# First expert network of a two-layer gated-attention kernel: gate and up accumulated over the experts in PSUM, down with tokens on the partitions, each token's expert picked by a per-token factor

## The chip, the cores and the metric

One core of one Trainium2 chip. The number is the device time of one execution in microseconds (us), the median of three.

## The reference

Two layers, each an attention over a context and then a feed-forward block, on 16 x 56 = 896 tokens of width 128. The change is in the feed-forward block of layer 0, a top-1 mixture of 8 routed experts and one shared expert, with inner width 256:

```python
logits = x @ gate_w
top_val = jnp.max(logits, axis=-1, keepdims=True)
top_id = jnp.argmax(logits, axis=-1)
xs = x * jax.nn.sigmoid(top_val)
g = jnp.einsum('th,ehi->eti', xs, rt_gate)
u = jnp.einsum('th,ehi->eti', xs, rt_up)
y = jnp.einsum('eti,eih->eth', jax.nn.silu(g) * u, rt_down)
routed = jnp.einsum('eth,te->th', y, one_hot(top_id, 8))
return silu(x @ sh_gate) * (x @ sh_up) @ sh_down + routed
```

The result is multiplied by tanh(g_ffn[0]) and added to the residual x. Then come the layer norm of layer 1 and its attention, whose queries are made from the normed x.

## The kernel before

Every engine runs an instruction list in the order in which the code writes it. The order is written out by hand, and semaphores (`sem(name)`) carry what one engine needs of another. Names: `pe` TensorE, `act` ScalarE, `dve` VectorE, `pool` GpSimd, `sp` the queue of the DMAs.

Numbers are kept as a float16 high part and a float16 low part (`g_split`, `u_split`, `d_split` for weights, `xs_split`, `xn_split`, `act_split` for data), so a product takes three matmuls: high with high, high with low, low with high. PSUM is `bank`, eight banks of 512 float32 columns.

Before the expert loop stands a head. PE turns the normed x (L747), makes the logits (L1028), and waits while DVE finds the one-hot row of each token. Then it turns the one-hot rows (L1034) and the scored x (L1038), and makes the query bias and output bias of layer 1 with 32 instructions of two columns or one (L1075, L1077).

The expert loop has two halves of the tokens (512 and 384). Within a half it goes over 8 routed experts and the shared one, and over 2 chunks of the inner width (`IC`): 36 units, numbered m. For a routed expert the tokens of the others are set to zero first. `hot_rows` (PE, L1049) spreads one row of the one-hot matrix over the partitions, `hot_mask_out` (ACT, L1391) copies it to SBUF, and `expert_tokens` (POOL, L723) multiplies it into the split x, giving `x_exp`, of which there are two. A unit is then:

- PE: 3 matmuls for gate and 3 for up (L1097), into banks 1, 2 or 3, 4 in turn;
- ACT: silu of the gate bank (L1422); DVE: times the up bank, from PSUM (L1754);
- ACT: high part of the product (`act_high`, L1397); DVE: low part, both inputs in SBUF (`act_low`, L1716);
- PE: 3 matmuls of `down` (L1061) for unit m - 2, issued behind gate and up of unit m, which accumulate in bank 5 (6 for the second half) over all units of the half.

The sum has features on the partitions. ACT copies it out (`block_out`), PE turns it back (L754), and DVE adds it to the residual (L1525). DVE also does the 13 steps `ternary` for the weights of a later network between units, and POOL makes the rstd of the layer norm (L576, L578).

Behind the loop PE makes the queries, 32 matmuls of 448 float32 columns (two instructions each, L1135), the first 16 for the first half of the tokens. ACT and DVE write each out as high and low (L1442, L1769). The norm of the last three token tiles and its turn (`pe_norm_half`) lie among the first 16. Then layer 1's scores begin (`pe_scores1`, L892).

## Time and profile before

| | |
|---|---|
| median of 3 runs | 1237.04 us (1234.59 to 1239.03) |
| the profiled execution's own time | 1237.67 us |
| its span in the trace | 1235.9 us |
| PE busy | 1121.8 us (91% of the span) |
| DVE busy | 890.4 us (72%) |
| ACT busy | 674.8 us (55%) |
| POOL busy | 519.8 us (42%) |
| PE busy from 500 to 600 us | 79.44 us of 100 |
| DVE busy from 500 to 600 us | 71.78 us of 100 |

Busy time is time in which the engine had an instruction under way; that of a matmul includes its passage through the array, so the sum of single durations is larger than the time they take in a row. PEclk is the clock granted to TensorE, 1.00 for 2.4 GHz and 0.50 for 1.2 GHz. The chain of waits is followed back from the last instruction: each piece is what the next one had been waiting for.

### The profile page before, as it was taken

The page shows a single profiled execution, that of the slowest core. Times are in us where ns is not written, and L with a number is a line of the kernel's source. Part 1 is how long each engine was busy: PE and PEld are TensorE (multiplying, and loading weights), DVE is VectorE, ACT ScalarE, POOL GpSimd, SP SyncE. Part 2 cuts the span into 40 slices and gives each one's busy share as a digit, 9 for nine tenths or more (in the row PEclk, how much of TensorE's full clock was granted, in tenths as well). Part 3 has the DMA queues.
Part 4 walks back from the last instruction along what each step waited for, and adds up shares of the span by engine and source line. Part 5 has one row for each costly group of instructions (what it writes and reads, how often), then busy time and mean ns, then how long its engine had stood idle before and what let it go on. Part 6 is the DMA issues. An engine that isn't in the chain of part 4 may idle for free.

```text
span 1235.9 us, 27523 instructions
## 1 busy us (share of the span) xinstructions
PE 1121.8 (91%) x9862; PEld 639.0 (52%) x9864; DVE 890.4 (72%) x1242; ACT 674.8 (55%) x935; POOL 519.8 (42%) x352
## 2 busy tenths in 40 slices
PE   4789999999999979878887999999999999999984
PEld 2255556566665645634433555555555555555542
DVE  7766666666666673587787887878787878878768
ACT  2345555555555545545575656656565656566532
POOL 8546675666666653432213332322232322323220
PEclk9889999999999999699998999999999999999996
DMA  3456555545555461000006887868776776768640
GB/s 105 121 169 197 169 168 165 156 149 160 157 178 158 145 159 47 20 1 26 2 0 130 161 164 142 158 140 163 137 163 144 156 162 141 159 141 160 131 79 16
DMA packets 247351, 157.59 MB, mean 128 GB/s; under 512 B 209664, under 2 KB 220400, under 8 KB 247296
## 3 DMA queue, kind: packets, MB, share of 16 engines
q1 hardware_dynamic: 247008, 156.86, 54.1%
q8 instruction: 34, 0.56, 0.2%
q14 instruction: 21, 0.17, 0.0%
q10 hardware_dynamic: 288, 0.00, 0.0%
HBM read 62.23 MB, written 25.39 MB: 71 GB/s over the span
## 4 chain that ended last, share of the span: by engine, by line
PE 73%; DVE 12%; issue 7%; ACT 6%; DMA 1%; SPq 0%; POOL 0%; ACTq 0%; DVEq 0%; another core or an unknown queue 0%; POOLq 0%
PE bank L892 16%; PE bank L912 15%; PE bank L767 7%; PE bank L791 6%; PE bank L860 5%; PE bank L795 5%; PE bank L808 4%; DVE region L1716 2%; PE bank L868 2%; PE bank L934 2%; DVE neg_max L1573 2%; ACT region L1242 2%; DVE e_row L1534 2%; PE bank L1135 2%; PE bank L1097 2%
## 5 line engine op out<-in xcount | busy, mean ns | idle before, releaser
L1534 DVE CUSTOM_DVE_ANT_0 e_row<-bank,region 112x1500 f32<-112x1500 f32 x128 | 220.1, 1719 | 125.5 <-PE bank L767 124.2
L1242 ACT ACTIVATE region<-bank 125x896 f32<-125x896 f32 x192 | 176.0, 917 | 203.8 <-PE bank L795 203.7
L1573 DVE TENSOR_REDUCE neg_max<-bank 128x1 f32<-128x1500 f32 x112 | 192.6, 1720 | 111.8 <-PE bank L892 111.8
L892 PE MATMUL bank<-region 128*128 128x500 f16 x1008 | 235.3, 379 | 3.2 <-ACT e_row L1269 1.8
L1269 ACT ACTIVATE e_row<-bank,neg_shift 128x1500 f32<-128x1500 f32 x112 | 169.2, 1511 | 101.0 <-DVE neg_shift L1577 58.4
L1278 ACT COPY region<-bank 128x768 f16<-128x768 f16 x192 | 152.4, 794 | 72.3 <-PE bank L860 72.3
L585 POOL CAST u_w<-e_row 128x1500 f16<-128x1500 f32 x56 | 83.0, 1483 | 209.4 <-ACT e_row L1269 179.2
L585 POOL CAST wg_sb<-e_row 128x1500 f16<-128x1500 f32 x56 | 83.1, 1484 | 192.4 <-ACT e_row L1269 128.4
L892 PEld LDWEIGHTS bank<-region 128*128 (+1 forms) x1008 | 97.4, 98 | 108.0 <-issue 3.5
L791 PE MATMUL bank<-row_of,region 112*128 112x448 bf16 x384 | 137.8, 359 | 7.6 <-ACT region L1242 7.6
L795 PE MATMUL bank<-region 97*128 (+1 forms) x768 | 137.6, 260 | 0.0
L912 PE MATMUL bank<-region 125*128 125x384 f16 (+1 forms) x576 | 126.1, 352 | 0.0
L912 PE MATMUL bank<-region,g_w 125*128 125x384 f16 (+1 forms) x576 | 124.8, 352 | 0.2 <-DMA region<-wg_sb 0.2
L646 POOL TENSOR_SCALAR region<-region 112x1500 bf16<-112x1500 int32 x16 | 105.3, 6583 | 35.3 <-PE bank L795 29.2
L767 PE MATMUL bank<-region 96*128 96x500 f16 x384 | 105.9, 385 | 12.5 <-DVE neg_max L1534 6.8
L808 PE MATMUL bank<-region 125*32 125x112 f32 x3072 | 113.1, 266 | 0.0
L795 PEld LDWEIGHTS bank<-region 97*128 97x128 f16 x768 | 76.0, 99 | 43.3 <-issue 0.9
L1600 DVE TENSOR_TENSOR u_w<-e_row,u_w 128x1500 f16<-128x1500 f32 x56 | 95.7, 1709 | 3.2 <-DMA region<-u_w 1.6
L1600 DVE TENSOR_TENSOR wg_sb<-e_row,wg_sb 128x1500 f16<-128x1500 f32 x56 | 95.5, 1706 | 3.1 <-POOL wg_sb L585 3.0
L808 PEld LDWEIGHTS bank<-region 125*32 125x32 f32 x3072 | 67.7, 109 | 41.0 <-issue 34.6
L912 PEld LDWEIGHTS bank<-region,g_w 125*128 125x128 f16 x576 | 52.8, 97 | 38.8 <-issue 1.3
L912 PEld LDWEIGHTS bank<-region 125*128 125x128 f16 x576 | 52.9, 97 | 38.5 <-issue 1.1
(218 smaller groups left out, 1495.3 us busy)
## 6 DMA issues: line engine op xcount, KB each, us to landing
region<-region SPq DMA_DIRECT2D x192, 96.0 KB, 2.2
turned_rows<-region SPq DMA_DIRECT2D x16, 768.0 KB, 3.8
region<-turned_rows SPq DMA_DIRECT2D x32, 384.0 KB, 3.5
c_in<-in_ctx SPq DMA_DIRECT2D x16, 750.0 KB
split_rows<-region SPq DMA_DIRECT2D x16, 750.0 KB
region<-in_mask_Bx1xSxS_if SPq DMA_DIRECT2D x32, 328.1 KB
region<-split_rows SPq DMA_DIRECT2D x24, 250.0 KB
g_w<-split_rows SPq DMA_DIRECT2D x24, 250.0 KB
```

The costliest lines, as they stand in the source:

```text
L585: pool.tensor_copy(halves1[(t + par) % 2][:, 0, :, 0:KP], e_row[(t + par) % 2][:].rearrange("p (c k) -> p c k", c=KC))\
L767: last = pe.matmul(bank[:, k, 0:4 * KP], q0_flat[0:96, bass.ds(b * ROWS + R0 * t, 128)], c_stack[par][0:96, t // 2, 4 * k:4 * k + 4, 0:KP] ...
L791: pe.matmul(into[:, 0:HALF_ROWS], mask_flat[par][:, KP * c:KP * c + 128], row_of[:].rearrange("p h s -> p (h s)"), start=True, stop=False)
L795: last = pe.matmul(into[:, GC * g:GC * (g + 1)], c_stack[par][0:97, 2 * h + g, c, :], q0[0:97, b, rows:rows + GC], start=False, stop=(g == 1))
L808: pe.matmul(bank[32 * j:32 * j + 32, U_BANK, 0:R0], c_pv[par][:, c, 4 * h + j, :], p0[:, c, R0 * j:R0 * (j + 1)], start=(c == 0), stop=False)
L892: last = pe.matmul(score_banks1(par, t)[:, k, :], q1[:, ql, b, 128 * t:128 * (t + 1)], c_t1[par][:, cl, 4 * k:4 * k + 4, 0:KP], start=(ql ...
L912: last = pe.matmul(bank[:, U_BANK, 0:cols], c_keep1[par][:, c, cl, :], p1[grp][0:KP, pl, c, :], start=(c == 0 and cl + pl == 0), stop=(c = ...
L1242: act.activation(p0[:, 2 * i:2 * i + 2, :], ring0("s", h, i)[0:KP, :, 0:HALF_ROWS], ACT.Exp, scale=SCALE0)\
L1269: act.activation(e_row[(t + par) % 2][:].rearrange("p (a k) -> p a k", a=3), score_banks1(par, t), ACT.Exp, bias=neg_shift[:, t:t + 1], ac ...
L1534: dve.tensor_tensor_reduce(out=masked.rearrange("p (a k) -> p a k", a=3), in0=bank[0:R0, 0:3, 0:4 * KP], in1=mask_bias[par][:].rearrange(" ...
L1573: dve.tensor_reduce(neg_max[:, t:t + 1], score_banks1(par, t), AX.XY, ALU.max, negate=True)\
L1600: dve.tensor_tensor(half[:, 1, :, 0:KP], e_row[(t + par) % 2][:].rearrange("p (c k) -> p c k", c=KC), half[:, 0, :, 0:KP], ALU.subtract).t ...
```

## The change

Units are now those of a half, of shared or routed, and of an inner chunk: 8 instead of 36 (`UNITS0`). The shared expert's four come first, two of them ahead of the turn of the one-hot rows. For the routed experts gate and up of all 8 experts accumulate in one pair of banks: only a token's own expert has a non-zero input, so the sum over the experts is that expert's value. silu, product, high and low part are done once for each of the 8 units. `x_exp` is released by a new semaphore, `x_used`.

`down` has the tokens on the partitions now: the product of one tile of 128 tokens is the stationary operand and the down weights of four experts (512 columns) move, then of four more, then of the shared one (128 columns). Each tile thus gets all experts' outputs in banks 5, 6 and 7, and DVE adds the right one to the residual with `pick`: nine dependent instructions for a tile, each multiplying 128 columns by a per-token factor (`hot_g`, zero but for the token's own expert). The four tiles of the first half are done in the second half's expert loop, the last three in the query phase. Copy, turn and addition of the old sum fall away.

```diff
         FFN_HALVES = [(0, 512), (512, NTOK)]
+        UNITS0 = [(half, shared, ic) for shared in (True, False) for half in range(2) for ic in range(IC)]
+        THIRDS = (2, 0, 1)
+        PICKS = NE + 1
+
+        def gate_bank(q):
+
+            return 1 + 2 * (q % 3)
+
+        def act_of(shared, half, ic):
+
+            return act_split[2 * half + ic if shared else 2 * IC + ic]
+
...
+
+            return bank[:, 7, 384:512]
...
             divide0(B - 1, 1, 1)
 
 
-            def low_weights(third):
...
                 a, z = FFN_HALVES[r // NE]
                 pool.wait_ge(sem("hot_mask"), r + 1)
-                if r >= 2:
-                    n = (r - 2) + (r - 2) // NE
-                    pool.wait_ge(sem("up0"), 2 * IC * (n + 1))
+                if r - 2 == NE - 1:
+                    pool.wait_ge(sem("up0"), 2 * 3 * IC)
+                elif r >= 2:
+                    pool.wait_ge(sem("x_used"), r - 1 - (1 if r - 2 >= NE else 0))
...
             for r in range(2 * NE):
-                if r == NE + 6:
-                    pool_rstd(pool, 2, 2 * TT, (0, 4))
                 expert_tokens(r)
+            pool_rstd(pool, 2, 2 * TT, (0, 4))
...
+            def gate_up(q, e, moving, first, last_e, name):
+
+                half, shared, ic = UNITS0[q]
+                a, z = FFN_HALVES[half]
+                if first:
+                    wait(pe, sem("act0"), q - 2)
+                for at, w in ((0, g_split), (1, u_split)):
+                    for wl, xl in ((0, 0), (0, 1), (1, 0)):
+                        last = pe.matmul(bank[:, gate_bank(q) + at, 0:z - a], w[:, e, wl, 128 * ic:128 * (ic + 1)], moving[xl],
+                                         start=(first and wl + xl == 0), stop=(last_e and wl == 1))
+                    if last_e:
+                        last.then_inc(sem("up0"), 1)
+                if name is not None:
+                    last.then_inc(sem(name), 1)
+
...
+            def down(t):
+
+                half = t // 4
+                pe.wait_ge(sem("act_low"), len(UNITS0) - 2 * (1 - half))
+                if t == 0:
+                    pe.wait_ge(sem("d_low"), 3)
+                tok = slice(128 * (t % 4), 128 * (t % 4 + 1))
+                products = [(ic, al, wl) for ic in range(IC) for al, wl in ((0, 0), (0, 1), (1, 0))]
+                for k in range(3):
+                    wait(pe, sem("picked"), PICKS * (t - 1) + (4, 8, 9)[k])
+                    for n, (ic, al, wl) in enumerate(products):
+                        if k < 2:
+                            last = pe.matmul(bank[:, 5 + k, :].rearrange("p (e h) -> p e h", e=4),
+                                             act_of(False, half, ic)[:, al, tok], d_split[:, 4 * k:4 * k + 4, wl, ic, :],
+                                             start=(n == 0), stop=(n == len(products) - 1))
+                        else:
+                            last = pe.matmul(shared_down(), act_of(True, half, ic)[:, al, tok], d_split[:, NE, wl, ic, :],
+                                             start=(n == 0), stop=(n == len(products) - 1))
+                    last.then_inc(sem("down0"), 1)
...
+            pe.wait_ge(sem("xn_t"), 4)
+            pe.wait_ge(sem("gu_low"), 2)
+            shared_unit(0)
             pe.wait_ge(sem("heads_sb"), 8)
+            shared_unit(1)
...
-                half, e = n // (NE + 1), n % (NE + 1)
...
-                for wl, al in ((0, 0), (0, 1), (1, 0)):
-                    last = pe.matmul(bank[:, 5 + half, 0:z - a], d_split[:, e, wl, ic, :], act_split[m % 3][:, al, 0:z - a],
-                                     start=(e == 0 and ic == 0 and wl + al == 0), stop=(e == NE and ic == IC - 1 and wl == 1))
-                last.then_inc(sem("down0"), 1)
...
-            for m in range(UNITS0):
-                n, ic = m // IC, m % IC
...
+            shared_unit(2)
+            hot_rows(1)
+            shared_unit(3)
+            for r in range(2 * NE):
+                half, e = r // NE, r % NE
                 a, z = FFN_HALVES[half]
...
-                wait(pe, sem("act0"), m - 1)
-                for w, at in ((g_split, 0), (u_split, 1)):
...
-                        moving = x_exp[(half * NE + e) % 2][:, xl, 0:z - a] if e < NE else xn_split[:, xl, a:z]
...
-                if m >= 2:
...
+                pe.wait_ge(sem("x_exp"), r + 1)
+                if half == 0 and e in (0, 3):
+                    pe.wait_ge(sem("gu_low"), 2 * (e // 3) + 4)
+                if r + 2 < 2 * NE:
+                    hot_rows(r + 2)
+                moving = [x_exp[r % 2][:, xl, 0:z - a] for xl in range(2)]
+                for ic in range(IC):
+                    gate_up(2 * IC + IC * half + ic, e, moving, e == 0, e == NE - 1,
+                            "x_used" if ic == IC - 1 and e < NE - 1 else None)
+                if r == 2:
                     pe.wait_ge(sem("bias1"), 2)
                     pe.wait_ge(sem("w_abs"), 3)
...
-                if m == 18:
+                if r == NE - 1:
                     turn_ternary(pe, 0)
                     turn_ternary(pe, 1)
-                if m == 20:
+                if r == NE:
...
-                if m == UNITS0 // 2 + 5:
+                if r == NE + 1:
                     pe.wait_ge(sem("w_t"), 3)
-                    pe_block_turn(pe, 2, range(4), in_bank_7)
-                if m == UNITS0 // 2 + 15:
-                    pe_norm_half(pe, range(4))
-            down(UNITS0 - 2)
-            down(UNITS0 - 1)
+                if NE + 1 <= r < NE + 5:
+                    down(r - NE - 1)
+            pe_norm_half(pe, range(4))
...
-                    pe.wait_ge(sem("act0"), UNITS0)
-                if n == 4:
-                    pe_block_turn(pe, 3, range(4, TT), in_bank_7)
+                    pe.wait_ge(sem("act0"), len(UNITS0) - 1)
+                if n == 2:
+                    pe.wait_ge(sem("act0"), len(UNITS0))
+                if n in (3, 5, 7):
+                    down(4 + (n - 3) // 2)
...
+            for n, (a, z) in enumerate(FFN_HALVES):
+                act.copy(xn_split[:, 0, a:z], bank[:, n, 0:z - a]).then_inc(sem("xn_t"), 1)
...
+
+            def silu_out(q):
...
+                act.activation(silu0[:, q % 2, 0:z - a], bank[:, gate_bank(q), 0:z - a], ACT.Silu, scale=1.0 / W_SCALE)\
...
+            def act_high(q):
+                half, shared, ic = UNITS0[q]
+                a, z = FFN_HALVES[half]
+                act.wait_ge(sem("act0"), q + 1)
+                if half == 1 and not shared:
+                    act.wait_ge(sem("down0"), 3 * 4)
+                act.copy(act_of(shared, half, ic)[:, 0, 0:z - a], act0[:, q % 2, 0:z - a]).then_inc(sem("act_high"), 1)
...
+            silu_out(0)
+            silu_out(1)
...
-            for m in range(UNITS0):
...
-                if m % IC == 0 and m // IC + 1 < 2 * (NE + 1):
-                    hot_mask_out(m // IC + 1)
-                if m >= 1:
-                    act_high(m - 1)
...
-                    block_out(0)
-                if m in (19, 21):
...
+            hot_mask_out(1)
+            for q in (2, 3):
+                silu_out(q)
+            for q in (2, 3):
+                act_high(q)
+            act.wait_ge(sem("in_down0"), 32)
+            act.wait_ge(sem("block_ready"), 1)
+            for r in range(2 * NE):
+                if r == NE:
+                    silu_out(4)
+                    silu_out(5)
+                if r + 2 < 2 * NE:
+                    hot_mask_out(r + 2)
+                if 1 <= r < 4:
+                    down_high(r - 1)
+                if r == NE:
+                    act_high(4)
+                    act_high(5)
+                if r in (NE - 1, NE):
+                    for n in ((0, 1), (2,))[r - NE + 1]:
...
+            dve.tensor_scalar(hot_g[:].rearrange("p t e -> p (t e)"), one_hot[:].rearrange("p t e -> p (t e)"),
+                              tanh_g[:, 2:3], 1.0 / W_SCALE, ALU.mult, ALU.mult).then_inc(sem("hot_g"), 1)
+            dve.tensor_scalar(shared_g[:], tanh_g[:, 2:3], 1.0 / W_SCALE, None, ALU.mult).then_inc(sem("hot_g"), 1)
...
+            def act_up(q):
+                a, z = FFN_HALVES[UNITS0[q][0]]
...
+                dve.scalar_tensor_tensor(act0[:, q % 2, 0:z - a], bank[:, gate_bank(q) + 1, 0:z - a], 1.0 / W_SCALE,
+                                         silu0[:, q % 2, 0:z - a], ALU.mult, ALU.mult).then_inc(sem("act0"), 1)
...
+            def act_low(q):
...
+                dve.tensor_tensor(split[:, 1, 0:z - a], act0[:, q % 2, 0:z - a], split[:, 0, 0:z - a],
+                                  ALU.subtract).then_inc(sem("act_low"), 1)
...
+            def down_low(third):
...
+            def pick(t):
...
+                dve.wait_ge(sem("residual"), TT + t)
+                if t == 0:
+                    dve.wait_ge(sem("hot_g"), 2)
+                for e in range(NE + 1):
+                    if e % 4 == 0:
+                        dve.wait_ge(sem("down0"), 3 * t + e // 4 + 1)
+                    if e > 0:
+                        dve.wait_ge(sem("picked"), PICKS * t + e)
+                    source, scale = (of(e), hot_g[:, t, e:e + 1]) if e < NE else (shared_down(), shared_g[:])
+                    done = dve.scalar_tensor_tensor(x_tok[:, t, :], source, scale, x_tok[:, t, :], ALU.mult, ALU.add)
+                    done.then_inc(sem("picked"), 1)
+                dve.wait_ge(sem("picked"), PICKS * (t + 1))
+                dve.sem_inc(sem("residual"), 1)
+
+            act_up(0)
+            act_up(1)
...
+            act_low(0)
+            act_low(1)
+            act_up(2)
+            act_up(3)
+            act_low(2)
+            act_low(3)
...
-            for m in range(UNITS0):
...
-                    ternary(m - 2)
-                if 6 <= m < 16:
-                    ternary(m - 3)
...
-                dve.scalar_tensor_tensor(act0[:, m % 2, 0:z - a], bank[:, 2 + 2 * (m % 2), 0:z - a], 1.0 / W_SCALE,
...
-                if m >= 1:
-                    act_low(m - 1)
-
-                if m == UNITS0 // 2 + 6:
-                    dve_residual(dve, TT + 4, 2, range(4), in_bank_7)
-                    dve_stats(dve, 2, range(4))
-                if m == UNITS0 // 2 + 12:
-                    dve_norm(dve, 2, range(4))
-            act_low(UNITS0 - 1)
+            for step in range(13):
+                ternary(step)
+                if step in (2, 5, 8):
+                    down_low(step // 3)
+            act_up(4)
+            act_up(5)
+            act_low(4)
+            act_low(5)
+            for t in range(4):
+                pick(t)
+            dve_stats(dve, 2, range(4))
+            dve_norm(dve, 2, range(4))
+            act_up(6)
+            act_up(7)
+            act_low(6)
+            act_low(7)
...
-                if n == 4:
-                    dve_residual(dve, 2 * TT, 2, range(4, TT), in_bank_7)
+                if n in (3, 5, 7):
+                    pick(4 + (n - 3) // 2)
+                if n == 7:
                     dve_stats(dve, 2, range(4, TT))
-                if n == 9:
+                if n == 11:
                     dve_norm(dve, 3, range(4, TT))
```

The instruction order around the three places that matter follows. On PE, in the first half of the expert loop, before; L1049 is `hot_rows`, L1097 gate and up, L1061 `down`:

```order
L1049 MATMUL bank<-one_hot_t,expert_row 128x512
L1097 MATMUL bank<-region 128x512 x6
L1061 MATMUL bank<-region 128x512 x3
L1097 MATMUL bank<-region 128x512 x6
L1061 MATMUL bank<-region 128x512 x3
```

and in the changed kernel (L1073 `hot_rows`, L1057 gate and up, L1099 a turn of ternary weights, L1088 and L1092 `down`), from the last expert of the first half on:

```order
L1057 MATMUL bank<-region 128x512 x12
L1099 MATMUL bank<-ident_b,g_w 128x128 x8
L1073 MATMUL bank<-one_hot_t,expert_row 128x384
L1057 MATMUL bank<-region 128x384 x12
L1099 MATMUL bank<-ident_b,g_w 128x128 x4
L1073 MATMUL bank<-one_hot_t,expert_row 128x384
L1057 MATMUL bank<-region 128x384 x12
L1088 MATMUL bank<-region 128x512 x12
L1092 MATMUL bank<-region 128x128 x6
```

No `down` stands between two experts of the first half any more; the first comes behind the second expert of the second half.

On PE in the head (L1028 then L1045 logits, L1034 and L1038 then L1109 and L1113 the two turns, L1057 the shared units), before:

```order
L1028 MATMUL bank<-gate_w_sb,x_norm_t 128x8 x7
L1034 MATMUL bank<-ident,one_hot 8x128 x7
L1038 MATMUL bank<-ident,x_norm 128x128 x7
L1049 MATMUL bank<-one_hot_t,expert_row 128x512
L1075 MATMUL bank<-bq_pad,region 128x2 x8
```

and now:

```order
L1045 MATMUL bank<-gate_w_sb,x_norm_t 128x8 x7
L1057 MATMUL bank<-region 128x512 x12
L1109 MATMUL bank<-ident,one_hot 8x128 x7
L1113 MATMUL bank<-ident,x_norm 128x128 x7
L1073 MATMUL bank<-one_hot_t,expert_row 128x512
L1119 MATMUL bank<-bq_pad,region 128x2 x8
L1121 MATMUL bank<-bv_col,region 128x1 x8
L1057 MATMUL bank<-region 128x384 x6
```

Two shared units of the first half stand between the logits and the turns; the two of the second half follow the biases.

On DVE from the end of the loop into the query phase (L1769, then L1850, is the low part of a query), before:

```order
L1716 TENSOR_TENSOR region<-region 128x384 x2
L1769 SCALAR_TENSOR_TENSOR region<-bank,q_bias,region 128x8x56 x5
L1525 SCALAR_TENSOR_TENSOR x_tok<-bank,tanh_g,x_tok 128x128 x3
L1509 BN_STATS stats<-x_tok 128x6 x3
L1512 BN_AGGR mean_var<-stats 128x2 x3
L1769 SCALAR_TENSOR_TENSOR region<-bank,q_bias,region 128x8x56 x5
```

and now (L1785 is `pick`; ahead of this piece stand the first four tiles' 36 picks and their norm):

```order
L1760 TENSOR_TENSOR region<-region 128x384 x2
L1850 SCALAR_TENSOR_TENSOR region<-bank,q_bias,region 128x8x56 x4
L1785 SCALAR_TENSOR_TENSOR x_tok<-bank,region,x_tok 128x128 x9
L1850 SCALAR_TENSOR_TENSOR region<-bank,q_bias,region 128x8x56 x2
L1785 SCALAR_TENSOR_TENSOR x_tok<-bank,region,x_tok 128x128 x9
L1850 SCALAR_TENSOR_TENSOR region<-bank,q_bias,region 128x8x56 x2
L1785 SCALAR_TENSOR_TENSOR x_tok<-bank,region,x_tok 128x128 x9
L1552 BN_STATS stats<-x_tok 128x6 x3
L1555 BN_AGGR mean_var<-stats 128x2 x3
L1850 SCALAR_TENSOR_TENSOR region<-bank,q_bias,region 128x8x56 x4
```

Three additions became 27 dependent picks in three packets, and the statistics moved from behind the fifth query to behind the eighth.

## Rows read from the trace of the kernel before

**Rows 1.** Busy time by engine, expert loop: window, PE, PEld, DVE, ACT, POOL, PEclk, DMA.
```profile
530.00:540.00 10.00, 7.62 (x34) 3.26 (x35) 8.13 (x13) 4.01 (x9) 2.57 (x2) 1.00 0.00 0
```

**Rows 2.** Chain of waits, 521 to 612 us: start, length, what.
```profile
521.32 4.75 PE bank L1097 x12
...
528.80 2.21 DVE region L1716
531.06 0.82 PE bank L1061 x3
531.88 0.32 PE bank L1049
532.20 0.77 PE bank L1097 x3
...
534.61 2.21 DVE region L1716
...
561.04 1.29 PE bank L1097 x6
...
605.30 0.97 PE bank L1097 x6
```

**Rows 3.** Groups by shape, 521 to 612 us: busy us, mean ns, idle before.
```profile
L1716 DVE TENSOR_TENSOR region<-region 128x512 f16<-128x512 f32 x18 | 23.4, 1300 | 1.6 <-ACT region L1397 1.2
...
L1422 ACT ACTIVATE region<-bank 128x512 f32<-128x512 f32 x18 | 10.7, 597 | 23.9 <-PE bank L1097 23.9
...
L1525 DVE SCALAR_TENSOR_TENSOR x_tok<-bank,tanh_g,x_tok 128x128 f32<-128x128 f32 x4 | 1.1, 335 | 0.0
...
L578 POOL TENSOR_TENSOR rstd<-rstd,half_neg 128x4 f32<-128x4 f32 x1 | 1.0, 1038 | 0.1
```

**Rows 4.** Timeline of DVE and POOL, 515 to 530 us: start, length, instruction.
```profile
515.44 4.60 DVE L1703 SCALAR_TENSOR_TENSOR region<-region 128x768 f16<-128x768 f32 x3
515.60 2.76 POOL L723 TENSOR_TENSOR region<-region 128x1024 f16<-128x1024 f16 x1 [6.38 <-DVE region L1698]
...
523.90 2.12 POOL L723 TENSOR_TENSOR region<-region 128x1024 f16<-128x1024 f16 x1 [5.54 <-ACT region L1391]
524.10 0.69 DVE L1754 SCALAR_TENSOR_TENSOR region<-bank,region 128x512 f32<-128x512 f32 x1 [0.93 <-PE bank L1097]
```

**Rows 5.** Busy time and granted clock (PEclk) in three short windows.
```profile
505.00:506.00 1.00, 1.00 (x7) 1.00 (x6) 0.00 (x0) 1.00 (x3) 1.00 (x2) 0.50 0.00 0
525.00:526.00 1.00, 1.00 (x4) 0.25 (x2) 0.00 (x0) 0.69 (x2) 1.00 (x1) 0.77 0.00 0
526.00:527.00 1.00, 1.00 (x6) 0.42 (x6) 0.82 (x2) 0.41 (x1) 0.02 (x1) 1.00 0.00 0
```

**Rows 6.** Timeline of PE ahead of the loop.
```profile
502.81 0.96 PE L747 MATMUL bank<-ident,x_norm 128*128 128x128 f32 x7 [1.98 <-issue]
...
510.19 1.65 PE L1034 MATMUL bank<-ident,one_hot 128*8 128x128 f32 x7 [2.83 <-DVE one_hot L1685]
...
513.80 3.57 PE L1075 MATMUL bank<-bq_pad,region 128*128 128x2 f32 x16
...
517.23 3.55 PE L1077 MATMUL bank<-bv_col,region 128*128 128x1 f32 x16
```

**Rows 7.** Timeline of two dependent DVE instructions, and of the seven-tile update.
```profile
509.58 0.21 DVE L1683 TENSOR_REDUCE first_top<-is_top 128x7 f32<-128x56 f32 x1
509.82 0.22 DVE L1685 TENSOR_TENSOR one_hot<-expert_id,first_top 128x56 f32<-128x56 f32 x1
...
495.12 1.90 DVE L1525 SCALAR_TENSOR_TENSOR x_tok<-bank,tanh_g,x_tok 128x128 f32<-128x128 f32 x7 [3.37 <-PE bank L754]
```

**Rows 8.** Chain of waits after the loop.
```profile
626.51 12.31 PE bank L1135 x32
...
640.25 2.10 PE bank L892 x9
...
653.65 0.51 PE bank L860 x6
```

More of the change, by code:

```diff
@@ new lines, in shared_unit, with hot_rows @@
+            def shared_unit(q):
+                a, z = FFN_HALVES[UNITS0[q][0]]
+                gate_up(q, NE, [xn_split[:, xl, a:z] for xl in range(2)], True, True, None)
+            def hot_rows(r):
+                half, e = r // NE, r % NE
+                a, z = FFN_HALVES[half]
+                wait(pe, sem("hot_mask"), r)
+                pe.matmul(bank[:, 0, 0:z - a], expert_row[:, e, :], one_hot_t[:, a:z],
+                          start=True, stop=True).then_inc(sem("hot_rows"), 1)
@@ L1031, in _, with turn_ternary @@
+            def turn_ternary(pe, n):
+                pe.wait_ge(sem("w_tern"), n + 1)
+                for j in range(JC):
+                    last = pe.transpose(tern_turned(n)[:, 128 * j:128 * (j + 1)], w_tern[:, n, j, :], ident_b[:])
+                last.then_inc(sem("w_turned"), 1)
+            pe.wait_ge(sem("xn_t"), 4)
+            pe.wait_ge(sem("gu_low"), 2)
+            shared_unit(0)
             pe.wait_ge(sem("heads_sb"), 8)
+            shared_unit(1)
             pe.wait_ge(sem("one_hot"), 1)
@@ L1033, in _ @@
             for t in range(TT):
-                last = pe.transpose(bank[0:NE, t // 4, 128 * (t % 4):128 * (t % 4 + 1)], one_hot[:, t, :], ident[:])
+                last = pe.transpose(bank[0:NE, 7 * (t // 4), 128 * (t % 4):128 * (t % 4 + 1)], one_hot[:, t, :], ident[:])
             last.then_inc(sem("hot_turned"), 1)
@@ L1134, in _ @@
                     pe.wait_ge(sem("q1_low"), n - 3)
-                pe.matmul(bank[:, n % 4, 0:HALF], a1_w[:, h, :], x_norm_t[:, HALF * half:HALF * (half + 1)],
+                pe.matmul(bank[:, 1 + n % 4, 0:HALF], a1_w[:, h, :], x_norm_t[:, HALF * half:HALF * (half + 1)],
                           start=True, stop=True).then_inc(sem("q1_made"), 1)
@@ L1366, in _, with hot_mask_out, down_high @@
             load_table(ACT.Silu)
-            act.wait_ge(sem("in_down0"), 32)
-            act.wait_ge(sem("block_ready"), 1)
-            for third in range(3):
+            def silu_out(q):
+                a, z = FFN_HALVES[UNITS0[q][0]]
+                act.wait_ge(sem("up0"), 2 * q + 1)
+                wait(act, sem("act0"), q - 1)
+                act.activation(silu0[:, q % 2, 0:z - a], bank[:, gate_bank(q), 0:z - a], ACT.Silu, scale=1.0 / W_SCALE)\
+                    .then_inc(sem("silu0"), 1)
+            def act_high(q):
+                half, shared, ic = UNITS0[q]
+                a, z = FFN_HALVES[half]
+                act.wait_ge(sem("act0"), q + 1)
+                if half == 1 and not shared:
+                    act.wait_ge(sem("down0"), 3 * 4)
+                act.copy(act_of(shared, half, ic)[:, 0, 0:z - a], act0[:, q % 2, 0:z - a]).then_inc(sem("act_high"), 1)
+            def hot_mask_out(r):
+                a, z = FFN_HALVES[r // NE]
+                act.wait_ge(sem("hot_rows"), r + 1)
+                wait(act, sem("x_exp"), r - 1)
+                act.copy(hot_mask[r % 2][:, 0:z - a], bank[:, 0, 0:z - a]).then_inc(sem("hot_mask"), 1)
+            def down_high(third):
                 part = slice(3 * third, 3 * third + 3)
@@ L1376, in _ @@
                 cols = 512 if n == 0 else NTOK - 512
-                last = act.copy(one_hot_t[:, 512 * n:512 * n + cols], bank[0:NE, n, 0:cols])
+                last = act.copy(one_hot_t[:, 512 * n:512 * n + cols], bank[0:NE, 7 * n, 0:cols])
             last.then_inc(sem("hot_t"), 1)
@@ L1670, in _ @@
             dve_norm(dve, 1, range(TT))
+            dve.wait_ge(sem("xn_t"), 2)
+            for n, (a, z) in enumerate(FFN_HALVES):
+                dve.tensor_tensor(xn_split[:, 1, a:z], bank[:, n, 0:z - a], xn_split[:, 0, a:z], ALU.subtract)\
+                    .then_inc(sem("xn_t"), 1)
             dve.wait_ge(sem("logits"), 1)
-            dve.tensor_copy(logits[:].rearrange("p t e -> p (t e)"), bank[:, 2, 0:TT * NE]).then_inc(sem("route"), 1)
+            dve.tensor_copy(logits[:].rearrange("p t e -> p (t e)"), bank[:, 7, 0:TT * NE]).then_inc(sem("route"), 1)
             dve.wait_ge(sem("route"), 1)
```

139 lines of the change are left out of this document (39 added, 100 removed).

## The prediction

> **What bounds the kernel now.** The change lies between 500 and 640 us, so I read that stretch and not the shares of the whole span. First the busy time by engine in a stretch of the expert loop [rows 1]: PE works 7.6 of 10 us and DVE 8.1, at the full clock. Neither is full, so something passes from one to the other and waits. Then the chain of waits [rows 2]. The loop's matmuls begin at 521.3 us. From there the chain repeats itself with each routed expert of the first half: DVE's `act_low` (L1716) begins at 528.80 and again at 534.61, a period of 5.81 us. Within it `act_low` takes 2.21 us, and `down` 0.82, the one-hot row 0.32 and half a unit 0.77 hang on it. Where PE is not held up it does six matmuls of 512 columns in 1.29 us (0.215 each) and six of 384 in 0.97 [rows 2]. So an expert needs of PE 3 x 6 x 0.215 + 0.32 = 4.2 us, and 1.6 of the 5.8 are waiting.
>
> Why is `act_low` long? Its mean is 1300 ns over 18, 23.4 us in all [rows 3]; seven at 2.2 us leave some 0.7 for each of the others. The long ones lie beside POOL's multiplication of the next expert's tokens, which takes 2.12 us [rows 4]. An instruction with only one operand in SBUF runs its 0.69 us in the middle of one (524.10 within 523.90 to 526.02) [rows 4]. Three DVE instructions with both operands in SBUF and one POOL instruction together took what they would one after another [rows 4]. DVE and POOL exclude each other for such pairs.
>
> After the loop PE makes the queries: the last 16 take 12.31 us, 0.77 each [rows 8], and layer 1's scores start at 640.25 [rows 8]. That start is what I forecast; after it the programs are alike.
>
> **The change part by part.** Columns on PE stay: gate and up are the same 216 matmuls, and `down` moves 7 x 6 x 1152 = 48,384 columns, as many as 18 x 3 x 896. The gain must come from waits, not from work.
>
> *Head.* Two shared units, 12 matmuls of 512 columns, now stand behind the logits. PE waits 2.83 us there for the one-hot rows [rows 6]. But the clock is at 0.50 (1.2 GHz) there [rows 5], so they take 12 x 512 columns at that clock = 5.1 us: 2.3 us too long for the gap. In return they are dense matmuls, and the one time the clock rose again here was after about 4 us of those: loop from 521.3 [rows 2], 0.77 in the window at 525 and 1.00 in that at 526 [rows 5]. Before that it had stayed at 0.50 through the turns and bias matmuls, in every window between those of the group. So I take it that it rises at the end of the two units. The seven turns (L1034) then cost 0.96 as L747 does at the full clock, not 1.65 [rows 6]: 1.3 us saved with the second seven. The 32 bias instructions take 7.0 us now, 0.22 each [rows 6]; from the turns' ratio, 3.8. Last bias at 520.8 + 2.3 - 1.3 - 3.2 = 518.6. The remaining two shared units (12 x 384 columns) and a row: I assume that the clock falls again during the biases, since it did not rise during them before, so 4.4 us at half speed. First routed expert at 523.0, from when the clock is whole. Bounds: never raised before 523, 527.5; kept, 518.6 + 2.2 = 520.8.
>
> *First half, 8 experts.* Nothing returns from ACT or DVE to PE between experts. PE needs 12 x 0.215 + 0.32 = 2.9 us for one. POOL's multiplication for expert r + 2 may start when r's matmuls are done, and has the 2.9 us of r + 1: 2.12 and some 0.3 for signals fit, by 0.5. DVE meanwhile does the 13 `ternary` steps and three `down_low`, which exclude POOL now and then; I add 1.0 us, and 0.2 for the sum over the weights. 23.2 + 1.2: end T = 547.4. Upper bound for this cost, every multiplication delayed by a whole DVE instruction of 0.87 (4.60 less the 2.0 in which POOL had it, by three) [rows 4]: 3.3 us an expert, 3 us more in all.
>
> *Turnover.* ACT stands before silu of the first sum in its own queue: it waits for eight ternary turns (0.7 us) and copies them out (two at 0.6, as [rows 3] has for 512 columns), then silu 0.6, DVE's product 0.69 [rows 4]. PE meanwhile has 0.26 + 0.97 and then must wait for the product, as the fourth pair of banks is the first again: 1.4 us. With 0.97, four turns, a row and 1.95 for the second expert: T + 7.1 = 554.5. The low parts are ready then, also with POOL once in the way.
>
> *Four tiles of `down` with three experts between.* A tile is 12 x 0.215 + 6 x 0.085 (six turns of 128 columns in 0.51 [rows 8]) = 3.1 us. An expert of the second half is 12 x 0.162 + 0.26 = 2.2. 12.4 + 6.6: 573.5. DVE's nine picks a tile depend on each other. One such instruction takes 0.335 us [rows 3], and a dependent one starts 0.03 after its predecessor ends (509.58 + 0.21, then 509.82) [rows 7]: 0.365, 3.3 us a tile. PE comes back to the same banks 2.2 us after leaving them, and the pick starts while PE is in the second bank, so this stays hidden.
>
> *To the queries.* Three experts, 6.4 us. POOL must do the last multiplication before the rstd of 1.04 us [rows 3], DVE the norm, PE four turns, ACT a copy: 1.3 us behind the experts. 581.2.
>
> *Queries.* 32 x 0.77 = 24.6 us, three tiles of `down` 9.3, the second norm's turn and copy 1.2, from the last query to the scores 1.4 (626.51 + 12.31 to 640.25 [rows 8]). And three new waits. DVE's list has the pick behind query 3, 5 and 7, PE's has `down` ahead of these queries and the next `down` waiting for four picks: PE stands 2.2 us before the second tile and 2.2 before the third. Then pick and statistics of the third hold back DVE's low parts, and PE waits 3.5 us for a bank at query 12. Sum 44.5 with small gaps. Scores at 625.7.
>
> 640.25 - 625.7 = 14.5 us less. The profiled execution took 1237.67, the median is 1237.04; I take it from the median: **1222.5**.
>
> The Trainium skill, "VectorE: DVE Perf Modes", section on the TRN2 errata, speaks against the picks: an instruction pays a fixed cost, from PSUM 120 cycles beside one per column, so tiles should have 512 columns or more. By that a pick would be 258 ns, which is the pitch of independent ones here (1.90 us for seven [rows 7]). For dependent ones the row of 335 ns decides, 23 us of DVE for 63 picks instead of 16.
>
> The skill's "SBUF - State Buffer", section "Who interferes with whom", says that an instruction of DVE with two SBUF inputs and one of GpSimd that reads SBUF exclude each other for their whole length. The trace agrees: 2.12 against 2.76 us for the same multiplication [rows 4]. By it no pick can be held up by POOL, since its source is in PSUM.
>
> **The rivals.**
>
> *The clock in the head comes out otherwise.* It does not rise early: +4.5, 1227.0, chance 0.15. For it: it stayed low for 20 us once. Or it rises and is kept: -2.2, and with fewer delays by DVE another -1, 1219.3, chance 0.15.
>
> *Picks overlap,* if a dependent one starts at the independent pitch of 0.26: 0.95 us a tile for the three tiles that PE waits for, -2.8, 1219.7. Chance 0.06; against it stand the dependent pairs.
>
> *POOL sets the pace of the first half* at 3.3 us an expert, and waits of PE on the one-hot rows come with it (each needs the mask before it copied, by an ACT that now also copies down weights): +3 to +5, 1226.5. Chance 0.08. For it: the margin is 0.5 us. Against it: DVE's list of such instructions is short.
>
> *The pick chain becomes the bound, and the kernel slower.* Its place is the second half, where a tile's chain stands against 5.3 us of PE, and the query phase, where PE waits for it. With a pitch p the query phase costs 27 (p - 0.365) more, and from p = 0.58 on the four tiles cost 36 (p - 0.58) more. The gain of 14.5 is gone at p = 0.72, twice the row; at 0.8 it is 5 us slower, 1242. For it: 63 instructions with a semaphore each, reading banks while PE writes their neighbours. Against it: L1754 reads PSUM under the same circumstances in its usual 0.69. Chance 0.05.
>
> *The buffers don't decouple:* if an expert's mask, multiplication and matmuls stay in series, 0.6 + 2.1 + 2.6 + signals is again 5.6 us and nothing is won in the first half: 1244 at worst. The order speaks against it, as the row for r + 2 is issued ahead of r. Chance 0.02.
>
> **How the numbers follow.** The forecast, 1222.5, has 0.49. Its own uncertainty is 3 us to each side. Down, the cases near 1219 with both small gains together reach 1216; up, the slow clock and the delays of POOL reach 1229. Between 1216 and 1229 I count some 0.8 of the chance. Below lie sums in which every wait is shorter, above the last two rivals. 0.3% of this kernel is 3.7 us, about what its measurement can tell from no change; to be within it the gain would have to lose 11 us, more than clock and POOL together. Faster 0.92, the same 0.03, slower 0.05.
>
> **What would show it.** In the changed trace: PEclk back at 1.00 before the biases; gate and up of the first half's experts at a period of 2.9 us with DVE and ACT no longer in the chain; one wait of some 1.4 us at the turnover; picks at a pitch of 0.365; PE waits of 2.2, 2.2 and 3.5 us among queries 5, 7 and 12; scores at 626. I am wrong if the period in the first half is over 3.3, if the query phase is over 50 us, or if the change shifts the clock's falls in layer 1 by more than 2 us.

## The result

The changed kernel takes 1222.38 us (median of 4, 1221.34 to 1223.59) against 1237.51 (median of 4, 1234.59 to 1239.03): ratio 0.9868, 95% interval 0.9826 to 0.9909, 15.1 us less; 1222.5 was forecast. The profiled execution has a span of 1219.7 us. PE is busy for 1116.7 us of it, DVE for 868.9 (890.4 before), ACT for 647.7 (674.8). All medians here leave out one slow execution, of `a_three_picks` (1875.6 us at a mean granted clock of 0.56).

The stretch of [rows 1] in the changed kernel (columns as there: window, PE, PEld, DVE, ACT, POOL, PEclk, DMA):

```profile
530.00:540.00 10.00, 9.97 (x45) 3.95 (x44) 9.90 (x9) 2.68 (x5) 7.53 (x4) 1.00 0.00 1
```

PE went from 7.6 of 10 us to 9.97. DVE reads 9.9, but it no longer holds PE up: part of that reading is its own waiting behind POOL, as the groups between 520 and 545 us tell (busy us, mean ns):

```profile
L741 POOL TENSOR_TENSOR region<-region 128x1024 f16<-128x1024 f16 x7 | 15.8, 2252 | 9.1 <-PE bank L1057 6.7 <-ACT region L1425 2.4
...
L1829 DVE TENSOR_SCALAR g_w<-g_w 128x512 bf16<-128x512 f32 x3 | 5.1, 1707 | 0.0
```

L1829 is the `ternary` step, which takes 0.43 us where POOL leaves it alone (the last of the three, at 543.72) and 2.35 us twice, beside POOL's multiplication. Nobody waits for it. POOL's multiplication has a mean of 2252 ns: five of the seven take 2.12 or 2.13 us, and two, beside DVE instructions with both inputs in SBUF, 2.54 and 2.60.

The chain of waits of the changed kernel, which answers to [rows 2] and [rows 8]:

```profile
501.00 0.64 PE bank L764 x4
...
505.54 4.87 PE bank L1057 x12
...
520.50 2.70 PE bank L1057 x12
523.20 0.32 PE bank L1073
523.52 2.70 PE bank L1057 x12
526.21 0.32 PE bank L1073
526.53 2.70 PE bank L1057 x12
...
544.40 0.46 PE bank L1099 x8
...
546.49 0.70 DVE region L1752
...
550.93 2.59 PE bank L1088 x12
...
569.59 0.26 PE bank L1073
...
577.56 2.52 PE bank L1170 x6
...
604.53 4.99 PE bank L1170 x8
...
624.34 2.10 PE bank L909 x9
```

No DVE or ACT piece stands between the experts, whose period is 3.01 us (520.50, 523.52, 526.53) against 5.81. DVE comes in once at the turnover (546.49). Read from the first turn of the normed x (501.00; 502.81 in [rows 6], 1.8 us earlier here, although the program up to there did not change: in the kept executions of this and the other kernels below it comes anywhere from 500.9 to 504.6), against the working of the prediction:

| us from the first turn | forecast | measured |
|---|---|---|
| last bias done | 15.8 | 15.3 |
| first routed expert | 20.2 | 19.5 |
| first half done (T) | 44.6 | 43.4 |
| first tile of `down` | 51.7 | 49.9 |
| four tiles done | 70.7 | 68.6 |
| first query | 78.4 | 76.6 |
| layer 1's scores | 122.9 | 123.3 |

In the kernel before the last was 137.4. So 14.1 us of the two spans' 16.2 come from the changed stretch. The 1.8 us before it are spread between executions, and from the scores to the end the two are 0.3 us apart (595.4 and 595.7).

### The profile page after: what moved, and what is told of

Read it like the earlier page. It is cut to its first block, busy times and chain, and to the rows that moved or that the text cites. A ratio compares the mean times of both kernels' runs of the same rounds, so it can differ in the third digit from the quotient of the medians.

```text
span 1219.7 us, 27431 instructions
## 1 busy us (share of the span) xinstructions
PE 1116.7 (92%) x9875; PEld 634.8 (52%) x9875; DVE 868.9 (71%) x1244; ACT 647.7 (53%) x878; POOL 520.5 (43%) x352
## 4 chain that ended last, share of the span: by engine, by line
PE 76%; DVE 10%; issue 7%; ACT 5%; DMA 1%; SPq 0%; POOL 0%; ACTq 0%; DVEq 0%; POOLq 0%
PE bank L909 16%; PE bank L929 16%; PE bank L784 7%; PE bank L808 6%; PE bank L877 5%; PE bank L812 5%; PE bank L825 4%; PE bank L1057 4%; DVE e_row L1577 2%; PE bank L885 2%; DVE neg_max L1616 2%; ACT region L1277 2%; PE bank L951 2%; PE bank L1170 2%; PE bank L855 2%
## 5 line engine op out<-in xcount | busy, mean ns | idle before, releaser
L784 PE MATMUL bank<-region 96*128 96x500 f16 x384 | 106.1, 386 | 12.3 <-DVE neg_max L1577 6.8
L812 PEld LDWEIGHTS bank<-region 97*128 97x128 f16 x768 | 76.0, 99 | 43.4 <-issue 0.9
```

What stands on the lines that cost most here:

```text
L784: last = pe.matmul(bank[:, k, 0:4 * KP], q0_flat[0:96, bass.ds(b * ROWS + R0 * t, 128)], c_stack[par][0:96, t // 2, 4 * k:4 * k + 4, 0:KP] ...
L812: last = pe.matmul(into[:, GC * g:GC * (g + 1)], c_stack[par][0:97, 2 * h + g, c, :], q0[0:97, b, rows:rows + GC], start=False, stop=(g == 1))
```

## Experiments

**The exclusion taken out of the kernel before** (`b_no_multiply`; part of the computation is left out):

```diff
-                pool.tensor_tensor(x_exp[r % 2][:, :, 0:z - a], xs_split[:, :, a:z], ...
+                c = z - a if r < 2 else 8
+                pool.tensor_tensor(x_exp[r % 2][:, :, 0:c], xs_split[:, :, a:a + c], ...
```

> The kernel before, with POOL's multiplication of the expert's tokens cut to 8 columns from the third on (the semaphores stay, most of x_exp keeps old data, so part of the computation is left out). Theory: the 1.6 us of waiting per expert in the first half is act_low shut out by that multiplication (2.21 us instead of 0.68). Then the period falls from 5.81 to about 4.3 us, all L1716 take 0.5 to 0.7 us, and the kernel takes 1217 us (7 x 1.5 + 8 x 1.2 = 20 less). Rival: the waiting is the round trip PE, ACT, DVE, PE itself; then the period stays over 5 us and the time over 1230 us.

1220.58 us, ratio 0.9831 (0.976 to 0.9902). The chain of waits for one expert:

```profile
526.18 0.32 PE bank L1050
526.50 1.40 PE bank L1098 x6
527.90 0.65 PE bank L1062 x3
528.55 1.29 PE bank L1098 x6
529.85 0.65 PE bank L1062 x3
530.49 0.32 PE bank L1050
```

PE follows PE; the period is 4.3 us, and act_low fell from a mean of 1300 ns to 686. 36 units, every silu and every low part, the round trip over three engines are still there. So that trip fits into PE's time, and the 1.6 us of waiting were POOL's: the cut takes its time and its exclusion together, and since no POOL piece stands in the chain of the kernel before [rows 2], it is the exclusion that counts. The gain is 17 us and not 20: where the second half makes the norm, the chain still goes over DVE (its updates, statistics and low parts, 573 to 578 us and 584 to 588 us in this kernel) in two of the experts.

**The same cut in the changed kernel** (`a_no_multiply`; same diff, part of the computation left out):

> The changed kernel with POOL's multiplication cut to 8 columns from the third on (part of the computation is left out). In the kernel before this same cut gave 17 us. Theory: the change had already taken that wait away, only some 1 us of POOL remains (the norm behind the last multiplication, one wait at an expert): 1221 us. Rival: the two are separate gains, and the cut is worth 17 us here too (1205).

1222.51 us, ratio 0.9873 (0.9806 to 0.9941): no change against 1222.4, though the four executions lie between 1218.2 and 1226.8. The trace is sharper. The first half lasts 23.8 us (23.9 with the multiplication), and from there to the first query it is 32.6 instead of 33.2: POOL is worth some 0.7 us here, and not 17. The two don't add up: the change had taken away the wait that the cut takes away.

**POOL's work doubled** (`a_double_multiply`):

```diff
-                pool.tensor_tensor(x_exp[r % 2][:, :, 0:z - a], ...
+                for twice in range(2):
+                    done = pool.tensor_tensor(x_exp[r % 2][:, :, 0:z - a], ...
+                    done.then_inc(sem("x_exp" if twice else "x_exp_once"), 1)
+                    if not twice:
+                        pool.wait_ge(sem("x_exp_once"), r + 1)
```

> The changed kernel with POOL doing each multiplication of the expert's tokens twice. Theory: an expert of the first half has 3.0 us of PE for 2.12 + 0.3 us of POOL; twice the multiplication is 4.3 + 0.3, so the period becomes 4.6 and PE waits for POOL in the first half, 7 x 1.6 us, and some 2 us in the last experts: 1235 us. Rival: PE doesn't follow POOL that closely because two buffers give it two periods; then under 1227 us.

1242.57 us (median of 10, 1235.65 to 1253.52), ratio 1.0034 (0.9994 to 1.0074), 20 us above the changed kernel where 13 were expected. POOL now is in the chain (start, length, what):

```profile
530.23 2.13 POOL region L742
...
534.50 2.13 POOL region L742
...
553.91 4.30 PE bank L1061 x12
```

The mechanism is as expected, and within the stretch the size nearly so: from the first turn to the scores it is 137.8 us instead of 123.3, 14.4 more. Of these the first half has 12.3 (36.2 instead of 23.9). Its period is 4.3 to 5.0 us, with a POOL that is itself held up beside DVE (its instructions take up to 2.72 us), and the clock is at 0.50 in the window from 554 to 556 us, so that the last expert of the half takes 4.30 us of matmuls instead of 2.7. The other 6 of the 20 us lie outside the stretch, 2.0 before it and 3.8 after the scores in this execution; nothing here shows why. The prediction's margin of 0.5 us is what this loop must keep: POOL's time beyond it comes back as time of the kernel.

**The shared units back behind the biases** (`a_shared_late`):

```diff
             last.then_inc(sem("logits"), 1)
-            shared_unit(0)
             pe.wait_ge(sem("heads_sb"), 8)
-            shared_unit(1)
             pe.wait_ge(sem("one_hot"), 1)
...
             pe.wait_ge(sem("xs_t"), 4)
+            shared_unit(0)
+            shared_unit(1)
             shared_unit(2)
...
-            silu_out(0)
-            silu_out(1)
...
+            silu_out(0)
+            silu_out(1)
             act_high(0)
```

ACT's silus move behind its copies with them, as shown, and DVE's two products (`act_up`) behind the low part of the scored x.

> The changed kernel, with the shared expert's first two units moved from between logits and turns to behind the bias matmuls. Theory: these two units fill PE's wait for the one-hot rows and bring the clock back before the turns and biases; without them turns and biases take 1.65 and 7.0 us again, and the first routed expert starts 6 us later than in the changed kernel: 1228.5 us. Rival: in front they cost as much as they save (5.1 us of half speed against a gap of 2.8), so the time stays within 2 us of 1222.4.

1227.7 us, ratio 0.9917 (0.9881 to 0.9952): 5.3 us more than the changed kernel. But this is a median between two groups: five executions took 1224.5 to 1225.7 us and five 1229.7 to 1237.0. All ten lie above 1224.4, which goes against the rival; that the total is 6 us more, no run shows. The kept trace is the fastest execution. Its chain:

```profile
508.24 1.65 PE bank L1107 x7
...
511.92 3.50 PE bank L1117 x16
515.42 3.41 PE bank L1119 x16
518.83 6.03 PE bank L1057 x18
...
610.61 3.29 PE bank L1170 x8
```

Turns 1.65 and biases 6.9 again, as in [rows 6]; the first expert starts 25.7 us after the first turn (526.58 less 500.86) instead of 19.5, so the 6 us are there in the head. The clock is at 0.50 in every window from 504 to 523 us, where the changed kernel has it at 1.00 from 510 to 516. From the start of the turns to the last bias it is 10.6 us against 5.9: 4.7 of the 6.2 us are the clock. The remaining 1.5 come from the two units no longer filling PE's wait.

The last line answers why this execution is only 3.0 us slower than the profiled one of the changed kernel (1224.49 and 1221.45). Those eight instructions come behind the same wait of 3.53 us in the query phase, but here the clock stays at 1.00 behind it and they take 3.29 us. In the chain of the changed kernel above they take 4.99.

**Matmuls that nobody needs, in the head of the kernel before** (`b_dummy_matmuls`):

```diff
             pe.wait_ge(sem("heads_sb"), 8)
+            pe.wait_ge(sem("gu_low"), 2)
+            for k in range(12):
+                pe.matmul(bank[:, 3, :]..., g_split[:, 0, 0, 0:128], g_split[:, 0], start=True, stop=True)
             pe.wait_ge(sem("one_hot"), 1)
```

> The kernel before with 12 matmuls of 512 columns into an unused bank put behind the logits; nothing uses their result. Theory: they last 5.1 us against a wait of 2.8, but bring the clock back before the turns and biases, so the last bias ends 2.5 us earlier than before and the kernel takes 1235 us in spite of more work. Rival: they cost what they exceed the gap by, 2.3 us: 1239.8.

1233.74 us, ratio 0.9959 (0.9926 to 0.9991): 3.9 us less with more work. The chain:

```profile
512.02 1.88 PE bank L1079 x16
513.90 2.90 PE bank L1081 x16
...
517.34 4.60 PE bank L1101 x12
```

The biases take 1.88 and 2.90 us instead of 3.50 and 3.41. In this execution PEclk is 1.00 in every window from 498 to 514 us: the clock did not even fall before the dummies, which start at 505.89 and take work off nobody, while in the kernel before it had fallen by 505 [rows 5]. So the expectation that they bring a fallen clock back was not put to the test. The last bias is done 14.6 us after the first turn instead of 18.0, and 1.1 of these 3.4 us come from the logits (1.71 us instead of 2.79), ahead of the dummies. That the dummies hold the clock through the turns is the likely reading, but not shown. For what the clock is worth in the head, and that two shared units bring it back, the run before is the evidence.

**The last three tiles' picks one query earlier** (`a_picks_early`):

```diff
-                if n in (3, 5, 7):
-                    pick(4 + (n - 3) // 2)
-                if n == 7:
+                if n in (2, 4, 6):
+                    pick(4 + (n - 2) // 2)
+                if n == 6:
                     dve_stats(dve, 2, range(4, TT))
-                if n == 11:
+                if n == 10:
```

> The changed kernel, with the picks of the last three tiles one query earlier in DVE's list (behind queries 2, 4, 6, statistics behind 6, norm behind 10); PE's list is the same. Theory: the waits of 2.2, 2.2 and 3.5 us on PE are an ordering of DVE's list, and the last one also lets the clock fall; all go, the query phase is 9 us shorter, 1213 us. Rival: the chain of nine dependent picks is itself what PE waits for; then it gains at most 2 us (1220).

1213.12 us, ratio 0.9773 (0.9702 to 0.9844), 9.3 us less than the changed kernel. First query and scores in the chain:

```profile
581.49 2.54 PE bank L1170 x6
...
619.46 2.10 PE bank L909 x9
```

and PE's timeline at the third tile of `down` and at the last wait of the first 16 queries:

```profile
592.82 2.75 PE L1088 MATMUL bank<-region 128*128 128x512 f16 x12
...
600.47 4.16 PE L1170 MATMUL bank<-x_norm_t,region 128*128 128x448 f32 x10 [1.50 <-DVE region L1850]
```

The query phase lasts 38.0 us instead of 46.8. The waits before the second and third tile are gone; the third wait is not, but shrinks from 3.53 to 1.50 us. With as many picks at the same pitch, it was the order of DVE's list that made them. Of the 8.8 us, 1.7 are the clock behind the last wait, which fell in the profiled execution of the changed kernel and did not in `a_shared_late` (45.1 us for the phase there).

**Three picks a tile instead of nine** (`a_three_picks`; other experts' outputs are left out):

```diff
                 for e in range(NE + 1):
                     if e % 4 == 0:
                         dve.wait_ge(sem("down0"), 3 * t + e // 4 + 1)
-                    if e > 0:
-                        dve.wait_ge(sem("picked"), PICKS * t + e)
+                        if e > 0:
+                            dve.wait_ge(sem("picked"), PICKS * t + e)
+                    else:
+                        dve.sem_inc(sem("picked"), 1)
+                        continue
```

> The changed kernel with only the first pick of each bank (three instead of nine a tile; the other experts' outputs are left out). Theory: in the second half of the loop nothing changes, since 3.3 us of picks hide behind 5.2 us of PE; in the query phase each of the two waits of 2.2 us shrinks by 1.1, the third by 2.5, and with it the clock may stay up (1.9): 1216 to 1218 us. Rival: picks cost nothing anywhere, 1222 us; or they bound the second half too, under 1210 us.

1215.37 us (median of 3, 1214.25 to 1216.32), ratio 0.9796 (0.9704 to 0.9887), 7.0 us less than the changed kernel and 0.6 below the expected range. Each of the first two waits is down to about 1 us:

```profile
587.45 2.75 PE L1088 MATMUL bank<-region 128*128 128x512 f16 x12 [1.04 <-DVEq L1785]
```

and the last to 1.23, the clock stays at 1.00, and the query phase lasts 40.0 us. The four tiles in the loop take 18.7 us as in the changed kernel. Two thirds of the picks gone bring less than the same picks one query earlier (40.0 against 38.0 us).

**Turnover mended as well** (`a_both`): besides the earlier picks, ACT copies the turned ternary weights out behind the two silus.

```diff
-                if r == NE:
-                    act_high(4)
-                    act_high(5)
-                if r in (NE - 1, NE):
-                    for n in ((0, 1), (2,))[r - NE + 1]:
...
+                for n in range(3) if r == NE else ():
+                    if n == 2:
+                        act_high(4)
+                        act_high(5)
+                    act.wait_ge(sem("w_turned"), max(n + 1, 2))
```

> The kernel with the picks one query earlier, and at the turnover ACT does silu of the first two sums before it copies the ternary turns out, so that PE's wait of 1.4 us for DVE's product goes. Theory: 1.2 us less than with the picks alone: 1212 us. Rival: the wait is the silu and product chain itself, no change (1213.1).

1213.27 us, ratio 0.9807 (0.9745 to 0.9869): the same as with the picks alone. The chain at the turnover:

```profile
546.84 0.45 PE bank L1099 x8
547.28 0.27 PE bank L1073
547.55 2.06 PE bank L1057 x12
549.61 0.22 PE bank L1099 x4
```

PE's wait for DVE's product is gone, but a wait of 0.28 us for the low parts follows, so from turn to first `down` it is 5.6 us instead of 6.5 (544.40 to 550.93). Less than 1 us can't be told from none in these times; in the traces it is 0.8 from first turn to scores (115.4 against 116.2).

## Why the prediction came out

*What bounds the kernel.* Right, and shown: `b_no_multiply` takes POOL's multiplication and with it the exclusion away and gets 17 us, and POOL itself stood nowhere in the chain. That the round trip over three engines sets the period by itself fell with it.

*Head.* Right in kind and size (15.3 against 15.8). The trace shows the clock at each of the assumed places (window, busy times, PEclk third from the end):

```profile
510.00:511.00 1.00, 1.00 (x9) 0.71 (x8) 0.98 (x2) 0.03 (x1) 0.00 (x0) 1.00 0.00 0
516.00:517.00 1.00, 1.00 (x8) 0.60 (x8) 0.00 (x0) 0.71 (x3) 0.39 (x1) 0.91 0.00 0
517.00:518.00 1.00, 1.00 (x3) 0.10 (x1) 0.83 (x2) 0.65 (x2) 0.00 (x0) 0.50 0.00 0
604.00:605.00 1.00, 0.47 (x1) 0.30 (x2) 1.00 (x3) 0.00 (x0) 0.92 (x2) 1.00 0.00 0
607.00:608.00 1.00, 1.00 (x2) 0.37 (x2) 1.00 (x3) 0.57 (x1) 0.00 (x0) 0.50 0.00 0
609.00:610.00 1.00, 0.83 (x5) 0.36 (x3) 0.68 (x1) 0.52 (x2) 0.00 (x0) 1.00 0.00 0
```

It is back at 510, at the end of the two shared units, as assumed. It falls again near the end of the window at 516 (0.91 there, 0.50 in the next), not in the biases as assumed but some 0.5 us behind the last of them (516.26), under the next shared unit. And it was back at 520, where the prediction has the first routed expert at full clock. This last part was in part luck. Five kept executions have the same code up to the end of that expert; they need 21.0 to 23.9 us to get there from the first turn (the changed kernel 22.2, the forecast makes it 22.8). In three of them (`a_picks_early`, `a_three_picks`, `a_both`) the clock came back only during it, and its twelve matmuls took 4.60, 4.25 and 4.26 us instead of 2.70.

*First half.* Period 3.01 against 2.9 plus an allowance: 23.9 us against 24.4. The term had a part that was too small and a reserve that was too large: the first six matmuls behind a one-hot row take 1.40 us, not 1.29 (also in the kernel before, in `b_no_multiply` above 526.50 and 528.55), and the 1.0 us for DVE's exclusions was hardly needed.

*Turnover and four tiles.* 6.5 for 7.1, with a wait of 1.05 us where 1.4 were forecast, and 18.7 for 19.0. DVE's picks hide there, as `a_three_picks` shows by leaving these 18.7 us as they are.

*Query phase.* Here the sum was 2.3 us too small, and the gains above, 1.8 us in all, nearly made it good. That errors of both signs cancelled so well is luck; the mechanisms were not. The waits are as written, from the timeline (start, length, and in brackets the idle time before):

```profile
585.13 3.57 DVE L1785 SCALAR_TENSOR_TENSOR x_tok<-bank,region,x_tok 128x128 f32<-128x128 f32 x9
...
586.77 2.99 PE L1088 MATMUL bank<-region 128*128 128x512 f16 x12 [2.20 <-DVE x_tok L1785]
...
593.86 2.99 PE L1088 MATMUL bank<-region 128*128 128x512 f16 x12 [2.20 <-DVE x_tok L1785]
...
604.53 4.97 PE L1170 MATMUL bank<-x_norm_t,region 128*128 128x448 f32 x8 [3.53 <-DVE region L1850]
```

2.20 and 2.20 us before the second and third tile of `down`, 3.53 before query 12. What the step lacked: in the last of these waits, 3.5 us with no matmul at all, the clock is lost (0.50 in the window at 607, above), and queries 12 to 15 take 4.97 us instead of 3.3. That is 1.7 of the 2.3 us, and it does not happen each time: of the four kept executions with this wait of 3.53 us the clock fell in or behind it in two (this one and `a_double_multiply`, 5.92 us) and stayed in two (`a_shared_late` and `a_no_multiply`, 3.27 each). And a pick has a pitch of 0.39 us (0.36 and 0.03), not 0.365: 3.57 a tile. By the prediction's own 27 (p - 0.365) this is worth an estimated 0.7 us, about the rest.

*The rivals.* The clock in the head came back where the forecast has it. Picks do not overlap: their pitch of 0.39 us is above both 0.26 and 0.365. POOL does not set the pace (3.01 us), but with its work doubled it does, so the rival's mechanism is real. The buffers decouple: the kernel would not have the same time with and without the multiplication otherwise. The slower one, the pick chain as the bound, had its place right, the query phase. What it costs depends on order and length together: the same picks one query earlier give 9.3 us, a third of the picks in the old order 7.0. The prediction took these waits (7.9 us of them in its sum) as a cost of the change; most of it (7.93 us of waiting, 1.50 with the picks earlier) was a cost of where the lists have the picks.

*The signs of being wrong.* None came up: the period is 3.01 us and not over 3.3, the query phase 46.8 and not over 50, and from the scores to the end the kernels differ by 0.3 us.

## What to carry to other kernels

Where two engines exclude each other, ask which of the excluded instructions somebody waits for, and take those off the path: without the multiplication that shut them out, the kernel before was 17 us faster. The whole rebuilding with fewer rounds over the other engines brought 15, and 24 once the order behind it was mended (1222.4 and 1213.1 us). When work is moved into another phase, read both engines' lists side by side: the same operation is free, or costs PE 2 us each time, according to which query DVE has it behind. And an idle stretch of PE can cost more than its length, when the clock falls behind it: 1.7 to 2.6 us more for one of 3.5 here, in two executions and not in two others, so one profile does not tell.

## What the runs showed of the hardware

- The clock can be low, and can fall, while PE reads as fully busy. First the kernel before in its biases, then the kernel with the dummies, where the clock falls within its matmuls of one column (513.90 to 516.80):

```profile
517.00:518.00 1.00, 1.00 (x6) 1.00 (x6) 1.00 (x1) 0.00 (x0) 1.00 (x1) 0.50 0.00 0
...
514.00:515.00 1.00, 1.00 (x9) 1.00 (x8) 1.00 (x2) 0.00 (x0) 1.00 (x1) 0.67 0.07 16
```

  PE is at 1.00 of 1.00 in both. At 0.50 such a matmul takes 0.21 us (3.41 by 16). In these traces the busy time does not tell whether the clock will hold.
- The same instructions behind the same wait of 3.53 us found the clock fallen in two kept executions and not in two others (4.97 and 5.92 us against 3.27 twice).
- Twelve matmuls whose result nobody uses made the kernel before 3.9 us faster (median of 10; the interval of the ratio, 0.9926 to 0.9991, ends close to none).
- DVE instructions with a single SBUF input are shut out by POOL too. Two rows of the changed kernel's timeline:

```profile
532.80 2.54 POOL L741 TENSOR_TENSOR region<-region 128x1024 f16<-128x1024 f16 x1 [1.31 <-PE bank L1057]
533.28 2.35 DVE L1829 TENSOR_SCALAR g_w<-g_w 128x512 bf16<-128x512 f32 x1
```

  2.35 us against 0.43 for the same step alone. The Trainium skill, "SBUF — State Buffer", section "Who interferes with whom", names such instructions (a tensor_scalar in a mode that uses both ports) beside those with two SBUF inputs; the prediction had counted only the latter, and the trace agrees with the page.
